# Layer 2 of a decoder: norm, router and sending of rows as one stage in four chunks instead of three stages in a row

## The reference

```python
logits = xf @ gate_w.T                      # xf = layernorm(x), 1024 x 128; gate_w 16 x 128
probs = jax.nn.sigmoid(logits)
top_vals, sel = jax.lax.top_k(probs, K)     # K = 2
weights = top_vals / (top_vals.sum(-1, keepdims=True) + 1e-06)
flat_sel = sel.reshape(-1)
onehot = jax.nn.one_hot(flat_sel, E, dtype=jnp.int32)
ranks = jnp.take_along_axis(jnp.cumsum(onehot, axis=0), flat_sel[:, None], axis=1)[:, 0] - 1
valid = ranks < capacity
slot = jnp.where(valid, flat_sel * capacity + ranks, sentinel)
padded = jnp.zeros((sentinel + 1, d), xf.dtype).at[slot].set(x_rep)   # each row twice
h = jax.nn.gelu(jnp.einsum('ecd,edf->ecf', padded, w1), approximate=False)
out_padded = jnp.einsum('ecf,efd->ecd', h, w2).reshape(sentinel, d)
out = (gathered * weights.reshape(-1)[:, None]).reshape(T, K, d).sum(axis=1)
```

## Time and profile before

| what | value |
|---|---|
| median of 3 runs | 1857.48 us (1857.1 to 1859.6) |
| profiled execution, its own time | 1858.08 us |
| its span, first to last instruction | 1856.2 us |
| PE busy | 1498.0 us, 81% |
| DVE busy | 857.5 us, 46% |
| ACT busy | 700.1 us, 38% |
| POOL busy | 483.3 us, 26% |

### The profile page before, as it was taken

One profiled execution on the slowest core, in us unless ns is written; L12 is line 12 of the kernel. 1 busy time (PEld: TensorE's weight loads), 2 busy tenths in 40 slices (PEclk: granted clock), 3 DMA queues, 4 the chain that ended last, 5 costly groups with the idle time before them and its releaser, 6 DMA issues. The chain is left out here.

```text
span 1856.2 us, 29632 instructions
## 1 busy us (share of the span) xinstructions
PE 1498.0 (81%) x10887; PEld 830.3 (45%) x10887; DVE 857.5 (46%) x2404; ACT 700.1 (38%) x1418; POOL 483.3 (26%) x566
## 2 busy tenths in 40 slices
PE   6899899995689999985998899973092579999876
PEld 4344344432544444454456344452071335555545
DVE  4555345542335555555312565355034645554244
ACT  2244414433137767562341143442031314343324
POOL 5533053310021111010001544100652435341034
PEclk9999999997999999986999999985595779999788
DMA  7800000000000000000002200000222000000012
GB/s 212 113 2 1 1 1 1 1 2 1 0 1 1 1 1 1 0 1 1 1 1 95 74 2 1 1 1 2 72 70 63 12 12 7 13 7 1 1 56 79
DMA packets 60258, 42.40 MB, mean 23 GB/s; under 512 B 13188, under 2 KB 54120, under 8 KB 60120
## 3 DMA queue, kind: packets, MB, share of 16 engines
q1 hardware_dynamic: 54752, 32.42, 7.1%
q0 software_dynamic: 3552, 7.33, 1.1%
q10 hardware_dynamic: 1816, 0.81, 0.2%
HBM read 25.88 MB, written 14.66 MB: 22 GB/s over the span
## 5 line engine op out<-in xcount | busy, mean ns | idle before, releaser
L1351 ACT ACTIVATE scores_L_experts_L<-L3x_psL 128x512 f32<-128x512 f32 x128 | 76.5, 597 | 173.2 <-PE L3x_psL L1214 169.5
L1388 DVE CUSTOM_DVE_ANT_0 L3x_junk<-L3x_psS,L3x_mask_rows 128x256 f32<-128x256 f32 x224 | 86.1, 421 | 92.4 <-PE L3x_psS L1176 84.0
L1214 PE MATMUL L3x_psL<-identb,L3x_mask_parts 128*128 128x256 bf16 x768 | 96.2, 276 | 0.0
L894 ACT ACTIVATE L0x_probs<-L0x_psL 128x512 f32<-128x512 f32 x96 | 52.1, 594 | 114.1 <-PE L0x_psL L707 78.9
L894 ACT ACTIVATE L2a_probs<-L2a_psL 128x512 f32<-128x512 f32 x96 | 52.1, 594 | 105.7 <-PE L2a_psL L705 70.9
L894 ACT ACTIVATE L0a_probs<-L0a_psL 128x512 f32<-128x512 f32 x96 | 52.1, 594 | 100.8 <-PE L0a_psL L705 65.0
L1196 PE MATMUL L3x_psL<-L3x_qm,ctx_T 32*128 32x512 f32 x256 | 73.3, 647 | 11.8 <-DVE L3x_mx L1388 11.3
L1214 PEld LDWEIGHTS L3x_psL<-identb,L3x_mask_parts 128*128 128x128 bf16 x768 | 70.4, 98 | 21.5 <-issue 13.7
L1625 PE MATMUL L1a_psL<-L1a_soft_near,neg_tri 128*128 128x512 f32 x128 | 67.9, 612 | 0.2 <-DVE L1a_soft_near L1832 0.2
L2907 POOL DMA_INDIRECT packed_rows<-h,slot x32 | 30.9, 964 | 141.7 <-POOLq L92 132.2
L1176 PE MATMUL L3x_psS<-L3x_km,L3x_qT 32*128 32x512 f32 x224 | 66.2, 668 | 1.9 <-DVE L3x_mx L1388 1.9
(11 more groups left out here) (800 smaller groups left out, 3917.6 us busy)
## 6 DMA issues: line engine op xcount, KB each, us to landing
L2f_rows<-packed_rows SPq DMA_DIRECT2D x8, 325.0 KB, 3.2
packed_rows<-zeros SPq DMA_DIRECT2D x1, 2560.0 KB, 28.2
experts_L_L<-in_L_ffn_w_dram SPq DMA_DIRECT2D x1, 2048.0 KB, 8.5
unpacked_rows<-zeros SPq DMA_DIRECT2D x1, 2048.0 KB, 18.0
scores_L_experts_L<-in_L_ffn_w_dram SPq DMA_DIRECT2D x1, 2048.0 KB, 7.9
L2f_back_rows<-unpacked_rows SPq DMA_DIRECT2D x16, 128.0 KB, 2.6
L3x_mask_rows<-in_mask_Bx1xSxS_ff_dram SPq DMA_DIRECT2D x8, 256.0 KB, 2.9
sorted_rows<-zeros SPq DMA_DIRECT2D x1, 1472.0 KB, 17.9
```

The costliest lines, as they stand in the source:

```text
L894: nc.scalar.activation(probs[:, half, a, k, :], psL[i % RING][:], ACT.Exp, scale=scale).then_inc(s_prob, 1)
L1214: last = nc.tensor.matmul(at[:, :, t * P:(t + 1) * P], parts[:, b % 2, i, t, u * P:(u + 1) * P], two, start=False, stop=i == PARTS - 1, sk ...
L1351: nc.scalar.activation(probs[:, half, a, k, :], psL[i % RING][:], ACT.Exp).then_inc(s_prob, 1)
L1388: last = nc.vector.tensor_tensor_reduce(out=junk[:, i, :], in0=psS[a][:, i * S:(i + 1) * S], in1=mrow[:, b % 2, t, :], scale=1.0, scalar=L ...
```

## The change

The first two stages and the sending half of the third become one stage, `send_to_slots`. Norm, transposes, router, choice of experts, ranks and slots now go chunk by chunk (four tiles each). The running count is kept in `ahead`, one row more than there are tiles, and carried from tile to tile. The waits on the count of a chunk, on its ranks and on its slots have semaphores that go up by one for each chunk. GpSimd sends the eight transfers of a chunk as soon as that chunk's slots and its second copy are there. The column of row numbers is now written by GpSimd at the stage's start. The two choices are handled in one instruction where there were two. The semaphore that counts landed transfers is now one of the whole program, and SP still waits for all 32 ahead of its first load. Line numbers behind the change: L2841 are the sends, L2896 and L2901 the norm, L2852 the transposes, L2857 the router, L2864 and L2865 the ranks and counts, L2906 to L2924 the choice, L2932 to L2942 the slots, L3001 SP's load.

```diff
+def send_to_slots(nc, mem, w, name, gate, rows, packed, scattered, E, capacity):
+    CHUNK = 4
+    CHUNKS = NT // CHUNK
...
             @block.gpsimd
             def _(pool):
+                nc.gpsimd.tensor_copy(rows[:, :, :, D], w["token"][:]).then_inc(s_ids, 1)
+                pool.wait_ge(s_ids, 1)
                 pool.wait_ge(w["zeroed"], 16 * len(blanks(w)))
-                for t in range(NT):
+                for c in range(CHUNKS):
+                    pool.wait_ge(s_twin, c + 1)
+                    pool.wait_ge(s_slot, c + 1)
+                    for t in range(c * CHUNK, (c + 1) * CHUNK):
                     for i in range(2):
                         nc.gpsimd.indirect_dma_start(packed, bass.IndirectOffsetOnAxis(ap=slot[:, i, t:t + 1], axis=0),
...
+            @block.tensor
+            def _(pe):
+                def route(c):
+                    pe.wait_ge(s_h, c + 1)
+                    if c >= 2:
+                        pe.wait_ge(s_hT, c - 1)
+                        pe.wait_ge(s_exp, c - 1)
...
+                    pe.wait_ge(s_hT, c + 1)
...
+                def rank_rows(c):
+                    pe.wait_ge(s_count, c + 1)
...
+                    nc.tensor.matmul(psK[c % 2][:, 0:CHUNK * E], w["earlier"][:], count[:], start=True, stop=True)
+                    nc.tensor.matmul(psK[c % 2][:, CHUNK * E:2 * CHUNK * E], w["ones"][:], count[:], start=True, stop=True).then_inc(s_ranked, 1)
+                route(0)
+                for c in range(CHUNKS):
+                    if c + 1 < CHUNKS:
+                        route(c + 1)
+                    rank_rows(c)
+            @block.scalar
...
+                for c in range(CHUNKS):
+                    act.wait_ge(s_turned, c + 1)
+                    nc.scalar.copy(hT[:, c * CHUNK * P:(c + 1) * CHUNK * P], psT[c % 2][:]).then_inc(s_hT, 1)
+                    act.wait_ge(s_h, c + 1)
+                    nc.scalar.copy(rows[:, 1, tiles(c), 0:D], rows[:, 0, tiles(c), 0:D]).then_inc(s_twin, 1)
+                    act.wait_ge(s_routed, c + 1)
+                    if c >= 1:
+                        act.wait_ge(s_count, c)
+                    nc.scalar.activation(probs[:], psR[c % 2][:, 0:CHUNK * E].rearrange("p (t e) -> p t e", e=E), ACT.Exp,
...
+            @block.vector
...
+                def place(c):
+                    dve.wait_ge(s_ranked, c + 1)
...
+                    for k in range(CHUNK):
+                        t = c * CHUNK + k
+                        steps.step(nc.vector.tensor_tensor(ahead[:, t + 1, :], ahead[:, t, :], counts[:, k, :], ALU.add))
...
+                steps.step(nc.vector.memset(ahead[:, 0, :], 0.0))
+                normal(0)
+                normal(1)
+                for c in range(CHUNKS):
+                    choose(c)
+                    if c + 2 < CHUNKS:
+                        normal(c + 2)
+                    place(c)
...
-                sp.wait_ge(s_scatter, 16 * 2 * NT)
+                sp.wait_ge(scattered, 16 * 2 * NT)
...
-            turn_and_route(nc, mem, w, "L2n", w["L2_ffn_gate_w"][:], 16, logits, h_all=rows[:, 0, :, 0:D])
-            slots_of_two(nc, mem, w, "L2r", logits, rows, slot, 16, capacity)
-            slot_experts(nc, mem, w, "L2f", rows, slot, w["L2_ffn_w1"], w["L2_ffn_w2"], w["packed"], w["unpacked"], 16, capacity)
+            send_to_slots(nc, mem, w, "L2n", w["L2_ffn_gate_w"][:], rows, w["packed"], scattered, 16, capacity)
+            slot_experts(nc, mem, w, "L2f", scattered, w["L2_ffn_w1"], w["L2_ffn_w2"], w["packed"], w["unpacked"], 16, capacity)
```

More of the change, by code:

```diff
@@ L2805, in sb, with ps @@
             return ctx.enter_context(nc.sbuf_tensor(f"{name}_{n}", shape, dt))
+        def ps(n):
+            return ctx.enter_context(nc.psum_tensor(f"{name}_{n}", [P, 512], F32))
         def sem(n):
             return sems(f"{name}_{n}")
[L2810 to L2817, removed]
-        with nc.Block() as block:
+        wide = [P, CHUNK, E]
+        hT = sb("hT", [P, NT * P])
+        probs, rest, equal, count = (sb(n, wide) for n in ("probs", "rest", "equal", "count"))
@@ new lines, in send_to_slots @@
+        one, both = sb("onehot", [P, 2, CHUNK, E]), sb("both", [P, 2, CHUNK, E])
+        val, key = sb("val", [P, 2, CHUNK]), sb("key", [P, 2, CHUNK])
+        total, rank, at, fits = sb("total", [P, CHUNK]), sb("rank", [P, 2, CHUNK]), sb("at", [P, 2, CHUNK]), sb("fits", [P, 2, CHUNK])
+        ahead, slot = sb("ahead", [P, NT + 1, E]), sb("slot", [P, 2, NT], U32)
+        psT, psR, psK = ([ps(f"{n}{i}") for i in range(2)] for n in ("psT", "psR", "psK"))
+        s_rstd, s_mean, s_h, s_turned, s_hT, s_routed, s_exp, s_twin = (sem(n) for n in (
+            "scales", "centred", "h_ready", "h_turned", "hT_ready", "routed", "exp_ready", "twin_ready"))
@@ L2821, in _ @@
                 act.preload_act_table_set("natural_log_exp_and_others")
[L2822 to L2831, removed]
+                nc.scalar.activation(mem.lnv[:], mem.mv[:, :, 1], ACT.Ln, bias=mem.eps[:]).then_inc(s_rstd, 1)
+                act.wait_ge(s_rstd, 1)
+                nc.scalar.activation(mem.rstd[:], mem.lnv[:], ACT.Exp, scale=-0.5).then_inc(s_rstd, 1)
+                for c in range(CHUNKS):
[7 more added lines that the diff above has]
+                    nc.scalar.activation(probs[:], psR[c % 2][:, 0:CHUNK * E].rearrange("p (t e) -> p t e", e=E), ACT.Exp,
+                                         scale=-1.0).then_inc(s_exp, 1)
             @block.vector
@@ L2842, in _ @@
[L2842 to L2859, removed]
+                desc = w["desc"][:, 0:E].unsqueeze(1).to_broadcast(wide)
@@ new lines, in best @@
+                def best(source, i):
+                    top, first = val[:, i, :].unsqueeze(2), key[:, i, :].unsqueeze(2)
+                    steps.step(nc.vector.tensor_reduce(top, source[:], AX.X, ALU.max))
+                    steps.step(nc.vector.tensor_tensor(equal[:], source[:], top.to_broadcast(wide), ALU.is_equal))
+                    steps.step(nc.vector.tensor_tensor(equal[:], equal[:], desc, ALU.mult))
+                    steps.step(nc.vector.tensor_reduce(first, equal[:], AX.X, ALU.max))
+                    steps.step(nc.vector.tensor_tensor(one[:, i, :, :], desc, first.to_broadcast(wide), ALU.is_equal))
```

73 lines of the change are left out of this document (53 added, 20 removed).

## The result

The changed kernel took **1841.66 us** (median of 4, 1840.74 to 1843.36) against 1857.81 for the kernel before on the same chip (median of 4, 1857.1 to 1859.6): ratio 0.9913, 95% interval 0.9896 to 0.9930, so 16.1 us faster. The forecast of 1837.8 was 3.9 us low, the range (1834.5 to 1843.5) holds the result, but in the part above 1840.5, which the prediction gave to rival 3 with a chance of 0.13. The profiled execution took 1840.74 us, its span is 1838.7, 17.5 less than before; it is the fastest of the four.

The account below looks back on a forecast made before the run. Bound: DVE's slots, then 32 sends at GpSimd's pace, then the load, one after another. First send 20.4 us earlier, less 0.5 at the end and 0.2 rounding: 19.7, so 1837.8 us from the median; range 1834.5 to 1843.5.

Parts of the forecast that it names:

- rival 3: Sending stage: sends stretched by 0.15 us each (1840.7) or 0.36 (1844.6), or chunk 1's slots late; chance 0.13 for above 1840.5.
- What bounds it, and the order of work: Stretch up to SP's load: three pieces run one after the other; the gain is what the first send moves ahead.
- The first send: Sending stage: chunk 0's slots at 1276.5, first send at 1276.75 against 1297.13, so 20.4 us earlier.
- DVE's chunks and GpSimd's slack: Sending stage: a chunk costs DVE 8.83 us, 7.5 for the last two; GpSimd never waits, 1.6 us to spare at the tightest.
- The end: Last send to SP's load: new stage end hidden behind the landing (2.33 against 2.30), or 1.07 on top; 0.5 lost taken.
- the 3.4 that the prediction had called wrong: Sign of being wrong: SP's load starting over 3.4 us behind the last send.
- Sends beside DVE: Overlap of sends with DVE work: no cost taken; bound 0.15 us for each of 19 sends, 2.9 us.
- Rivals 1: Sending stage: sends stand still while DVE works, all 32 go from 1300.6, kernel takes 1861.5; chance 0.04.
- Rival 2: Sending stage: DVE's steps with two SBUF inputs stand still while a send runs, 12.4 us lost, 1850.2; chance 0.05.
- Rival 4: Experts' start: PE's clock rise may come at another point, 3 us either way; chance 0.04 for under 1834.5.

Follow-up runs that it names:

- late_sends: Changed kernel, but GpSimd waits for slots and second copies of all four chunks before its first send: 1888.39 us, ratio 1.0025.
- chunk2: Changed kernel with chunks of 2 tiles in place of 4 (8 chunks): 1873.87 us, ratio 0.9945.
- after_again: The changed kernel run once more, unaltered, on a slower chip: 1871.88 us, ratio 0.9935 to the kernel before.
- drain: Changed kernel, but GpSimd waits before the sends of chunks 1, 2 and 3 until all earlier sends have landed: 1872.22 us, ratio 0.9939.
- best_pause: `best` plus one GpSimd pause before chunk 1's sends until the eight sends of chunk 0 have landed: 1867.89 us, ratio 0.9907.
- best: Changed kernel with SP's first three loads inside the sending stage and chunk c's slots ahead of chunk c + 2's norm: 1869.57 us, ratio 0.9924.

## Why the prediction was right

- **What bounds it, and the order of work.** Right: `late_sends` shows that nothing but the moved first send brings the gain.
- **The first send.** 20.4 forecast, 20.1 measured. The counts of chunk 0 stood at +11.56 (forecast +11.76), the slots at +16.32 (+16.71); DVE's 64-wide steps took 0.22 and went every 0.257. From the slots to the send it was 0.91 and not 0.27. The earlier trace rows is a send of results, which comes 0.28 behind DVE in the changed kernel too, although it is the first of its stage there; a send for whose slots GpSimd stood waiting came 0.76 behind them at every later border (`chunk2`, `after_again`). What makes those slower was not tested. The two misses have opposite signs (0.39 early, 0.64 late), so the first send is nearer to its forecast than its parts.
- **DVE's chunks and GpSimd's slack.** Forecast 8.83, then 7.5; measured 8.54, then 7.96 and 8.13. The wait for ranks with its cover gone was 0.80 twice, where I said some 0.5. It cost nothing, as the slack took it. Chunk 1's slots were there 2.4 us before GpSimd was free for them (1283.37 against 1286.08 less its own 0.30), where I had 1.6.
- **The end.** This is the step that was wrong: "0.5 lost", with a bound of 1.07. It was 2.07, and the load came 4.37 behind the last send, past the 3.4 that the prediction had called wrong. The sum took GpSimd's leaving to be like DVE's in the earlier trace rows, 1.07, and it is 3.4 behind indirect transfers. The question I left open (does the barrier wait for the landing?) has the answer no, and wasn't the one that mattered.
- **Sends beside DVE.** Taken as nothing, and so it was: 0.95 to 0.97 long, every 1.26 us, the one exception 1.01. Rivals 1, 2 and 3 fall on the result's chip. The time lies in the region of rival 3 all the same, put there mostly by the stage's end, for which the range above 1840.5 had not been made; that the range holds the result is in this respect luck. Rival 2's direction, DVE held up by sends, is real on the slower chips, though not as I priced it: in this stage nothing is late there up to the 12th send.
- **The clock.** Rival 4's 3 us were not seen. PE started on the experts at 1322.82 with a granted clock of 0.50; it was 0.50 from 1329 to 1330, 0.78 from 1330 to 1331 and 1.00 from then on, so the rise came some 7.6 us behind the start. Before, it was 0.60 from 1348 to 1349 and then 1.00, 6.8 us behind a start at 1341.99. Those 0.8 us more at half the clock are worth 0.4 us (an estimate), about the 0.45 that the experts' start took more.

Of the 3.9 us between forecast and median, 1.6 is the stage's end, 0.3 the first send, 0.1 the pace and 0.45 the experts' start, less the 0.2 that the sum had taken off for rounding: 2.2 in all. The other 1.6 lies mostly in how far the profiled executions are from their medians (0.9 under it behind the change, 0.6 over the median of three before), over which the two traces say nothing.

## What to carry to other kernels

Where one engine makes a list and another works it off at its own pace, the gain of overlapping them is what the first item moves ahead, and it holds only while the maker keeps up: at two tiles a chunk DVE's fixed cost per step made it the bound, at eight the first item came late. A stage end that is newly put behind work has to be priced by the engine that leaves last and by what it did last; rows of another engine don't give it. And issue what follows within the same stage: three loads moved ahead of the barrier started 2.30 us behind the last send again, though in the kernel's time the gain was not clear of the noise.

## What the runs showed that I had not expected

- With GpSimd's last indirect transfer as the last work of a stage, the next stage starts 3.4 us behind its end (3.42, 3.43), and 3.58 behind the landing if GpSimd waits for that; with its memset it is 0.73, and with DVE's work 10 us behind the sends 0.99, in the very same stage. What GpSimd does in that time was not found.
- On three other chips DVE's steps in this stage come late, on a grid of 0.70 us, once 12 or 13 indirect sends have gone in one unbroken run, and are on time again some 4 us behind the start of its last send. On the result's chip 19 sends beside DVE do nothing of the sort. Breaking the run ends it (`drain`, `best_pause`), but what is held up in the meantime was not found: the trace names "remote", "issue" or the step before. Those chips are also slower in the kernel before (1884 against 1858), and the trace of `pool_last`, that kernel with one memset more, shows where. Up to its first send of results it is within 0.2 us of the trace of the kernel before; by the end of that stage it is 10.4 behind, and it loses 15.4 more from layer 3's sends to the end, which is all of the difference in span (1882.0 against 1856.2). In the changed kernel the time from the first send of results to SP's load of them is 61.8 us there against 51.6. Beside the sends of results it isn't DVE alone that is late, nor does it take 12 sends: four instructions of ACT that go every 0.5 us on the result's chip start there with 4, 6, 7 and 8 sends out:

```profile
1361.34 0.44 ACT L3001 ACTIVATE L2f_hidden<-L2f_psU 128x320 f32<-128x320 f32 x1 [3.22 <-issue]
1363.73 0.44 ACT L3001 ACTIVATE L2f_hidden<-L2f_psU 128x320 f32<-128x320 f32 x1 [1.96 <-PE L2f_psU L2957]
1364.46 0.44 ACT L3001 ACTIVATE L2f_hidden<-L2f_psU 128x320 f32<-128x320 f32 x1 [0.29 <-remote]
1365.89 0.44 ACT L3001 ACTIVATE L2f_hidden<-L2f_psU 128x320 f32<-128x320 f32 x1 [0.99 <-remote]
```

The last distances, 0.73 and 1.43, are nearly those of DVE's late steps. That it is one effect is likely by this, but no run tested it, and from which send on it begins has no single number.
- The first send of the sending stage takes 1.19 us (1.47 in `best` and `best_pause`) and not 0.96; behind a pause in `drain`, and as the first of the experts' stage, a send takes 0.96. A pause for the landing costs 1.8 us, not 1.1, since the next send starts 0.8 behind the landing.
